# A selective scan run in place over tiles that alternate in direction, with layer norm on ScalarE and GpSimd and the products with C in pairs

## The reference, cut to what matters

```python
xn = (xf - mu) / sqrt(var + EPS) * ln_g + ln_b          # layer norm over 64 channels
xz = x @ in_proj_w.T;  xi, z = split(xz)
u = silu(causal_conv4(xi) + conv_b)
dt, Bm, Cm = split(u @ x_proj_w.T)
delta = softplus(dt * dt_proj_w + dt_proj_b)
for t in range(L):                                      # L = 56 * 56 pixels of an image
    h = h * exp(delta[t] * A) + (delta[t] * u[t]) * B[t]   # h: channels x 16 states
    y[t] = sum over states of h * C[t]
out = x + ((y + u * D) * silu(z)) @ out_proj_w.T
```

## Time and profile before

| | |
|---|---|
| median of 3 runs | 9379.95 us (9377.71 to 9384.65) |
| profiled execution | 9385.57 us, span 9383.8 us |
| busy, share of the span | PE 83%, DVE 74%, ACT 57%, POOL 58% |
| Mamba stage | first scan at 721.2 us, last at 7038.8 us |
| operations of the Mamba loop | 3584 scans, 3584 drives, 3584 decays, 3584 products |
| memset of `hs` ahead of the loop | 6.03 us on VectorE |

### The profile page before, as it was taken

One profiled execution on the slowest core, in us unless ns is written; L12 is line 12 of the kernel. 1 busy time (PEld: TensorE's weight loads), 2 busy tenths in 40 slices (PEclk: granted clock), 3 DMA queues, 4 the chain that ended last, 5 costly groups with the idle time before them and its releaser, 6 DMA issues. The chain is left out here.

```text
span 9383.8 us, 134613 instructions
## 1 busy us (share of the span) xinstructions
PE 7771.6 (83%) x30601; PEld 4082.9 (44%) x30601; DVE 6973.6 (74%) x9361; ACT 5322.5 (57%) x9326; POOL 5475.1 (58%) x4944
## 2 busy tenths in 40 slices
PE   9977777787777778777777777777778999999996
PEld 9962222222222222222222222222225899959996
DVE  7759999999999999999999999999991122212222
ACT  0237777777777777777777777777770133201432
POOL 0008888888888888888898888888880000000000
PEclk9988888888888888788887888888889999999998
DMA  9646565655655656555665565656651000030002
GB/s 175 168 122 167 159 166 162 165 163 162 166 163 165 163 162 166 163 164 164 164 167 162 163 164 165 166 161 166 163 162 56 17 0 0 18 86 0 0 0 55
DMA packets 1108342, 1202.02 MB, mean 128 GB/s; under 512 B 460432, under 2 KB 1094800, under 8 KB 1107344
## 3 DMA queue, kind: packets, MB, share of 16 engines
q1 hardware_dynamic: 871568, 1117.24, 44.2%
q10 hardware_dynamic: 236032, 77.08, 3.6%
HBM read 961.04 MB, written 155.41 MB: 119 GB/s over the span
## 5 line engine op out<-in xcount | busy, mean ns | idle before, releaser
L644 POOL TENSOR_TENSOR prod<-hs,bsp 128x448 f32<-128x448 f32 x3584 | 4067.8, 1158 | 647.1 <-PE ps L655 464.1
L632 DVE TENSOR_TENSOR_SCAN hs<-da,hs,ps 128x448 f32<-128x448 f32 x3072 | 3490.8, 1136 | 0.0
L623 DVE TENSOR_TENSOR ps<-ps,bsp 128x448 f32<-128x448 f32 x3585 | 2186.6, 610 | 249.1 <-PE ps L607 223.0
L607 PE MATMUL ps<-stack,seld 96*128 96x448 bf16 x3587 | 1422.2, 411 | 1054.8 <-DVE hs L632 1001.9
L613 ACT ACTIVATE da<-da,nega 128x448 f32<-128x448 f32 x3588 | 2235.9, 661 | 16.0 <-issue 7.2
L906 PE MATMUL ps<-pv,ws 128*128 128x224 f32 x8800 | 1692.3, 354 | 9.4 <-ACT pv L1064 7.0
L906 PEld LDWEIGHTS ps<-pv,ws 128*128 128x128 f32 x8800 | 1657.3, 189 | 45.0 <-issue 7.7
L655 PE MATMUL ps<-prod,wc 128*32 128x448 f32 x7200 | 1551.4, 719 | 90.3 <-POOL prod L644 86.7
L607 PEld LDWEIGHTS ps<-stack,seld 96*128 96x128 bf16 x3587 | 347.8, 99 | 2660.5 <-DVE hs L632 2338.2
L1237 DVE SCALAR_TENSOR_TENSOR pv<-ps,R 128x224 f32<-128x224 f32 x880 | 422.4, 480 | 1279.0 <-PE ps L906 1279.0
L407 PE MATMUL ps<-xn,wtap 128*128 128x448 f32 x1808 | 982.3, 650 | 3.5 <-ACT bsp L467 3.5
(11 more groups left out here) (118 smaller groups left out, 7223.8 us busy)
## 6 DMA issues: line engine op xcount, KB each, us to landing
da<-delta_copy SPq DMA_DIRECT2D x3595, 224.0 KB, 3.6
stack<-parts SPq DMA_DIRECT2D x2700, 28.0 KB, 2.3
delta_copy<-dlt SPq DMA_DIRECT2D x225, 224.0 KB, 1.9
lnx<-in_x SPq DMA_DIRECT2D x118, 224.0 KB, 3.7
lny<-y_nchw SPq DMA_DIRECT2D x118, 224.0 KB, 4.3
x_column_pairs<-otile SPq DMA_DIRECT2D x225, 116.0 KB, 2.7
xpad<-x_column_pairs SPq DMA_DIRECT2D x32, 812.0 KB, 4.3
xpad<-in_x SPq DMA_DIRECT2D x64, 392.0 KB, 6.8
```

The lines of the kernel that those rows point to most:

```text
L607: pe.matmul(ps[:, DU_BANK + j % 4, 0:T], seld[0:96, b, :], stack[:, st.t % 2, grp, :], start=True, stop=True).then_inc(S["du_spread"], 1)
L623: v.tensor_tensor(du, du, bsp[:, st.t % 2, 0, :], ALU.mult).then_inc(S["dbu_done"], 1)
L632: v.tensor_tensor_scan(hs[:, j, :], da[:, j % SLOTS, :], ps[:, DU_BANK + j % 4, 0:T], 0.0 if first else hs[:, j, T - 1:T], ALU.mult, ALU.add)\
L644: g.tensor_tensor(prod[:, j % 8, :], hs[:, j, :], bsp[:, st.t % 2, 1, :], ALU.mult)\
```

## The change

Four things are changed in the Mamba stage.

1. The scans run in place: `hs` is gone, `da` has 16 slots of 449 columns, and the state takes the place of the decays. Every second tile (odd t) lies backwards in time, so that the last state of a tile is the column next to where the following tile begins. A scan runs over 449 columns from 1.0: its first column takes over the state left by the tile before (a zeroed PSUM column is its drive). What TensorE reads for a backward tile (`xn` for the taps and `z`, `yg` for the projection) is read backwards.
2. A load of decays waits for the product of the same unit in the tile before, not for a scan.
3. Layer norm leaves VectorE: ScalarE applies scale and shift (`ln_affine`), GpSimd adds (`ln_sum`) and multiplies by `rstd` (`ln_scale`), and gain and bias go into ScalarE's last step.
4. GpSimd multiplies two units by C in one instruction, at odd steps; some steps of the tables move.

```diff
-ACT_AT = {2: ["relu", "cast0"], 4: ["cast1"], 5: ["silu", "u", "z", "exp"], 6: ["evacuate"], 7: ["lnc"], 8: ["bc0"],
-          9: ["dt"], 10: ["dt2", "bc1"], 11: ["lnv"], 13: ["clamp"], 14: ["shift"]}
-DVE_AT = {0: ["add_x"], 3: ["gate"], 11: ["scale"]}
-POOL_AT = {1: ["rest0"], 4: ["rest1"], 9: ["over"], 12: ["delta"], 13: ["delta_u"]}
-SP_AT = {1: ["copy"], 7: ["part0"], 10: ["part1"], 12: ["part2"], 13: ["store"]}
+ACT_AT = {0: ["scale_y"], 2: ["cast0"], 3: ["relu"], 4: ["cast1"], 5: ["silu", "u", "z", "exp"], 6: ["evacuate"],
+          7: ["lnc"], 8: ["bc0"], 9: ["dt"], 10: ["dt2", "bc1"], 11: ["lnv"], 13: ["clamp"], 15: ["shift"]}
+DVE_AT = {3: ["gate"]}
+POOL_AT = {1: ["rest0", "add_x"], 5: ["rest1"], 9: ["over"], 11: ["delta"], 13: ["delta_u", "times_rstd"]}
+SP_AT = {1: ["copy"], 5: ["part0"], 7: ["part1"], 9: ["part2"], 12: ["store"]}
...
-            da = sb(m, "da", [P, SLOTS, T])
-            hs = sb(m, "hs", [P, UN, T])
+            da = sb(m, "da", [P, UN, T + 1])
...
+        def span(buf, a, n, back):
+            return buf[:, a + n - 1:a - 1 if a else None:-1] if back else buf[:, a:a + n]
+        def elements(j, t):
+            lo = 0 if t % 2 else 1
+            return da[:, j, lo:lo + T]
+        def drives(bank, lo=1, hi=T + 1):
+            return ps[:, DU_BANK + bank, lo:hi]
...
-                sp.wait_ge(S["x_summed"], st.ln)
+                sp.wait_ge(S["x_relu"], st.ln)
...
-        def ln_sum(v, st):
-            v.wait_ge(S["ln_loaded"], (st.ln + 1) * 32)
-            if not (st.ahead and st.k == 0):
-                v.wait_ge(S["x_relu"], st.ln)
-            v.scalar_tensor_tensor(xsum[:, :], lny[:, :], col(SCALE2), lnx[:, :], ALU.mult, ALU.add)\
-                .then_inc(S["x_summed"], 1)
+        def ln_affine(a, st):
+            a.wait_ge(S["ln_loaded"], (st.ln + 1) * 32)
+            a.activation(lny[:, :], lny[:, :], ACT.Identity, bias=col(SHIFT2), scale=col(SCALE2)).then_inc(S["y_scaled"], 1)
+        def ln_sum(g, st):
+            g.wait_ge(S["y_scaled"], st.ln + 1)
+            g.tensor_tensor(lnx[:, :], lnx[:, :], lny[:, :], ALU.add).then_inc(S["x_summed"], 1)
...
-            a.activation(xres[:, :], xsum[:, :], ACT.Relu, bias=col(SHIFT2)).then_inc(S["x_relu"], 1)
+            a.activation(xres[:, :], lnx[:, :], ACT.Relu).then_inc(S["x_relu"], 1)
...
-            v.scalar_tensor_tensor(xg[:, :], xcen[:, :], vec_c(0), xrstd[:, :], ALU.mult, ALU.mult)\
-                .then_inc(S["scaled"], 1)
+        def ln_scale(g, st):
+            g.wait_ge(S["rstd"], st.ln + 1)
+            g.tensor_tensor(xcen[:, :], xcen[:, :], xrstd[:, :], ALU.mult).then_inc(S["scaled"], 1)
...
-                sp.wait_ge(S["scan_done"], (st.tile - 1) * UN + (j + 9))
+                sp.wait_ge(S["prod_done"], st.tile * UN + (j + 1))
...
-            v.wait_ge(S["prod_done"], n + 1)
-            first = st.t % KT == 0
-            v.tensor_tensor_scan(hs[:, j, :], da[:, j % SLOTS, :], ps[:, DU_BANK + j % 4, 0:T],
-                                 0.0 if first else hs[:, j, T - 1:T], ALU.mult, ALU.add)\
-                .then_inc(S["scan_done"], 1)
+            h, bank = da[:, j, :], j % 4
+            if st.t == 0:
+                a, d, start = h[:, 1:T + 1], drives(bank), 0.0
+            elif st.t == KT:
+                a, d, start = h[:, T - 1::-1], drives(bank, 1, T + 1)[:, ::-1], 0.0
+            elif st.t % 2:
+                a, d, start = h[:, ::-1], drives(bank, 1, T + 2)[:, ::-1], 1.0
+            else:
+                a, d, start = h, drives(bank, 0, T + 1), 1.0
+            v.tensor_tensor_scan(a, a, d, start, ALU.mult, ALU.add).then_inc(S["scan_done"], 1)
...
-            g.wait_ge(S["scan_done"], n + 9)
+            g.wait_ge(S["scan_done"], n + 10)
...
-            g.tensor_tensor(prod[:, j % 8, :], hs[:, j, :], bsp[:, st.t % 2, 1, :], ALU.mult)\
-                .then_inc(S["prod_done"], 1)
+            lo = 0 if st.t % 2 else 1
+            g.tensor_tensor(prod[:, j % 8:j % 8 + 2, :], da[:, j:j + 2, lo:lo + T],
+                            bsp[:, st.t % 2, 1:2, :].to_broadcast([P, 2, T]), ALU.mult).then_inc(S["prod_done"], 2)
...
-                        times_c(g, st, j)
+                        if j % 2:
+                            times_c(g, st, j - 1)
```

More of the change, by code:

```diff
@@ L192, in build @@
             "y_summed", "y_gated", "out_mm", "out_evac", "out_stored0", "out_stored1")}
-        spread_in = [sem(f"c_spread_in{i}") for i in range(SLOTS)]
+        spread_in = [sem(f"c_spread_in{i}") for i in range(16)]
         D = {n: sem("d_" + n) for n in (
@@ L406, in conv_tap @@
             a = st.far_k * T + k
-            mm = pe.matmul(ps[:, TMP_BANK + bank, 0:T], wtap[:, st.far_s, k, :], xn[:, a:a + T],
+            mm = pe.matmul(ps[:, TMP_BANK + bank, 0:T], wtap[:, st.far_s, k, :], span(xn, a, T, st.back),
                            start=(k == 0), stop=(k == 3))
@@ L415, in emit @@
                     a = st.far_k * T + 3
-                    return pe.matmul(o, wcs("gate_in", st.far_s, P), xn[:, a:a + T], start=True, stop=True)
+                    return pe.matmul(o, wcs("gate_in", st.far_s, P), span(xn, a, T, st.back), start=True, stop=True)
             elif name == "dt":
@@ L606, in spread_du @@
             pe.wait_ge(S["scan_done"], st.tile * UN + j + 5)
[L607 removed]
+            pe.matmul(drives(j % 4), seld[0:96, b, :], stack[:, st.t % 2, grp, :],
                       start=True, stop=True).then_inc(S["du_spread"], 1)
         def decay(a, st, j):
[L612 to L613 removed]
+            a.wait_ge(spread_in[j], st.tile * 16 + 16)
+            a.activation(elements(j, st.t), elements(j, st.t), ACT.Exp, scale=nega[:, j:j + 1])\
                 .then_inc(S["exp_done"], 1)
@@ L671, in project_out @@
                 o = ps[lo:lo + C, O_BANK, 0:T // 2]
-                pe.matmul(o, wcs("proj_out", 0, C), yg[:, odd:T:2], start=True, stop=False)
+                y = yg[:, T - 1 - odd:None if odd else 0:-2] if back else yg[:, odd:T:2]
+                pe.matmul(o, wcs("proj_out", 0, C), y, start=True, stop=False)
                 mm = pe.matmul(o, wcs("residual", s, C), xn[:, 3 + k * T + odd:3 + k * T + T:2], start=False, stop=True)
@@ L857, in _ @@
             sum_states(pe, tile, 3)
-            project_out(pe, tile, s, k)
+            project_out(pe, tile, s, k, par == 1)
             barrier(pe, 3)
@@ L1010, in _ @@
                                 evacuate(a, tile, par, before)
+                            elif name == "scale_y":
+                                if st.has_ln:
+                                    ln_affine(a, st)
                             elif name == "relu":
@@ L1117, in _ @@
                 v.sem_inc(S[f"out_stored{par}"], 16)
-            for k in range(6):
-                st = Ahead(k)
-                ln_sum(v, st)
-                ln_scale(v, st)
             for j in range(LEAD["drive"]):
@@ L1131, in _ @@
                         for name in DVE_AT.get(j, ()):
-                            if name == "gate":
-                                gate(v, tile, ub)
-                            elif name == "add_x":
-                                if st.has_ln:
-                                    ln_sum(v, st)
-                            elif st.has_ln:
-                                ln_scale(v, st)
+                            gate(v, tile, ub)
             tile, ub, s, k, par, before, img = ended(PAIRS, 0)
@@ L1254, in _ @@
             g.wait_ge(S["ready"], 4)
+            for k in range(6):
+                st = Ahead(k)
+                ln_sum(g, st)
+                ln_scale(g, st)
             st = Ahead(0)
@@ L1275, in _ @@
                                 delta_times_u(g, st)
-                            else:
+                            elif name.startswith("rest"):
                                 rest_of(g, st, int(name[4]))
+                            elif st.has_ln:
+                                if name == "add_x":
+                                    ln_sum(g, st)
+                                else:
+                                    ln_scale(g, st)
             barrier(g, 3)
```

34 lines of the change are left out of this document (14 added, 20 removed).

## The result

The changed kernel takes 9417.4 us (median of 7; 9409.3 to 9432.1), the kernel before beside it 9384.7 us: a ratio of 1.0037 (95% interval 1.0025 to 1.0049). It is slower, by 33 us where I had forecast 190.

A forecast was written before the change was run, and what follows sets the result against it. It took a ring of waits between ScalarE and GpSimd as the bound: seven plain tiles at 26.1 and seven layer-norm tiles at 32.0 us, +11.6 a pair of images, +192 with the start, about 9570 us (9404 to 9748).

The forecast's parts named there:

- The ring: ScalarE and GpSimd, in program order, wait for each other: 12.24 us cast to `over`, 14.28 back, setting a tile without layer norm.
- plain tile: Tile without layer norm, seven in a pair of images; forecast 26.1 us with four pairs of products, a gain of 0.5.
- layer-norm tile: One of tiles 8 to 13 and 0; forecast 32.0 us against 29.9 before, a loss of 2.1.
- relu to cast: ScalarE's relu, the decay behind it and a handoff, newly on the ring in layer-norm tiles: 1.2 us.
- One sign: Expected in the profile if right: ScalarE's relu waiting some 5 us for GpSimd's `add_x`.
- q = 2.10: Price in us of one GpSimd instruction multiplying two units: two products at 1.10 less a fixed part; bounds 1.96 and 2.32.
- the upper side: Reasons for a pair price near 2.32 us: the pair's second dimension and its starts at odd columns.
- 304.3 + 49q: Time in us of a pair of images as a function of q, the price of a pair of products.
- Item 3: Layer-norm tile, from the end of `dq` to `delta` by TensorE's sum, two pairs and `over`: 4.35 us, lower bound 3.8.
- rival 4: Gain and loss cancel, q near 1.85 to 1.9, no change in time; chance 0.04.
- Backward scans: Rival: backward scans or drives are dear, 1.30 us instead of 1.075, a backward tile 28.3, kernel 9710; chance 0.08.
- the rival had 8615: Rival: VectorE sets the end after all, every tile takes its 24.8 us, kernel 8615; chance 0.05.

The follow-up runs named there:

- b_const: The kernel before with every scan started from 0.0, so no state is carried from tile to tile; 9368.7 us, ratio to before 0.9984.
- a_best: a_early with a separate buffer for the scaled chunk, GpSimd's product by rstd after unit 3 and ScalarE's shift after unit 14; 9039.5 us, ratio to before 0.9626.
- a_dt_relu: a_dt with ScalarE's relu moved from unit 9 to unit 6, ahead of `dt`; 8680.4 us, ratio to before 0.9249.
- a_unroll: The changed kernel with two pairs of images in one pass of the loop, 8 passes in place of 16; 9387.6 us.
- a_late: The changed kernel with GpSimd's product by rstd and ScalarE's shift one tile later; 9383.9 us, ratio to before 1.0002.
- a_early: a_late with `scale_y`, `add_x` and SP's loads for them one tile earlier; 9362.8 us, ratio to before 0.998.
- a_lnv: The changed kernel with layer norm back on VectorE, scans and pairs as in the change; 9387.2 us, ratio to before 1.0001.
- a_lnv_late: a_lnv with VectorE's scaling and ScalarE's shift one tile later; 9266.9 us, ratio to before 0.9875.
- a_dt: a_best with work on `dt` ahead of layer norm's relu, centring and squares, `scale_y` and `add_x` back in the relu's tile; 9026.3 us, ratio to before 0.9611.
- a_single: The changed kernel with one GpSimd product an instruction instead of pairs; 9491.1 us, ratio to before 1.0114.
- a_forms: The changed kernel plus GpSimd products of several shapes timed on zeros ahead of the loop; one row 1126 ns, two rows 2068 ns.

## Why the prediction was wrong in size

**The ring was right.** Cast to `over` 12.25 us (12.24 forecast); plain tile 17.72 + 4 × 1.90 = 25.3 against 25.4 measured. In the layer-norm tile shown: relu to cast 1.05 (1.2), cast to the end of `dq` 13.6 (13.5), from there to `delta` 3.8 (4.35; 4.3 in the tile before it). From the end of the squares to the first pair behind TensorE's sum it took 3795.08 − 3790.35 = 4.73 us, against 4.74 before. b_const, a_best and a_dt_relu show the mechanism by taking it apart: cheaper scans bought 16 us, another order of the same work 737. As a sum the ring is less sure: a_unroll, a_best and a_dt_relu came out near what it gave (a_dt_relu 35 us below), while a_late, a_early, a_lnv, a_lnv_late and a_dt gained 79 to 213 us less, and a_single cost 161 less. One sign came out weak: the relu waits 1.7 to 1.9 us for `add_x`, where I had named some 5; the long wait is GpSimd's 6.92 for the sum.

**The step that failed is the price of the pair, q = 2.10.** Its pitch is 1.90 (3.65 to 3.98 for two), below even my lower bound of 1.96. The parts, from runs: two products at 1.10 are 2.21; one fixed part less, 184 ns where I took 98 from a memset; and 0.15 less because one row of a pair, on average, starts at a cheap column, a saving of the new layout for which I had no term. 2.21 − 0.18 − 0.15 = 1.88. The repeated row of C, my reason for a low bound, brings nothing, and the odd starts, one of my reasons for the upper side, are what makes half the rows cheaper.

**Two more errors, which nearly cancel.** The forecast's formula, 304.3 + 49q, gives 397.4 us a pair of images at 1.90, close to the 396.6 measured, and 49 × 0.20 × 16 = 157 us is close to the 153 by which the time was missed. That closeness is luck. Item 3 of the forecast holds the price of two further pairs, which the formula leaves at 2.10; at 1.90 the item is 3.95, a layer-norm tile 31.05 and a pair of images 7 × 25.32 + 7 × 31.05 = 394.6, against 394.9 in the mean before: no change. Tiles 8 to 13 bear this out with 30.91. What made the kernel slower is tile 0, 33.06 for 31.05: ScalarE's wait at the loop's jump, which the sum put at nothing (a_unroll, 31.13 without the jump). 2.0 × 16 = 32 us, of the 33 measured; the rest cancels within a few microseconds, the start among it (4.8 us for 7). So the time lies within my range of 9404 to 9748 by luck, too. It lies nearest to rival 4, no change with q at 1.85 to 1.9, which I gave 0.04.

**The count of pairs is too large as a rule.** Going back to single products raises the price by 0.14 us a pair; over 49 pairs that should cost 110 us, over 63 (with item 3's) 141. It cost 74, in the main because in the layer-norm tiles `over`, and so the sum that it stands behind, came sooner (a_single). The agreement above holds for the waits of this kernel alone.

**The rivals.** Backward scans are not dear: 1078 ns in both directions. VectorE's floor of 24.8 us a tile is real, but only another order reaches it: a_dt_relu comes to 8680 where the rival had 8615. The rule of the Trainium skill, Perfetto Trace Analysis, section "Identifying the Most-Contended Engine", would have begun with VectorE, the busiest engine of the plain tiles before. b_const disagrees, 26.45 us a plain tile with cheaper scans.

## What to carry to other kernels

When two engines that work in program order hand work back and forth inside a tile, write down the ring and price what lies on it; the busy shares say little until the ring is broken. A step that is moved off the ring brings its own waits to the place where it lands, so look at what its input waits for there. Price a merged instruction by measuring the fixed part on that engine, and look at what the new layout does to the price, too: sort the times of one instruction by row before taking their mean.

## What the runs showed of the hardware

- GpSimd multiplies a row of 448 columns that starts at a multiple of four columns in 1126 to 1134 ns (a_forms, before); a straight line through 224 and 448 columns leaves 186 ns of it fixed. A row that starts two or three columns behind a multiple of four takes 977 ns (a_single). Two rows in one instruction take 1770, 1927 or 2080 ns with two, one or none of the cheap kind (after).
- VectorE's scaling, with two SBUF inputs, takes 653 ns in the median where it is placed after unit 5 (a_lnv_late) and 1965 ns where it meets GpSimd's pairs (a_lnv); in one such tile it ended 0.5 us after the pair. Its longest was 1689 ns among single products (before) and 2337 among pairs. The Trainium skill, SBUF — State Buffer, section "Who interferes with whom", describes an exclusive lock on a pair of ports that VectorE and GpSimd share. These rows agree with it: the excess over 683 ns, 1.01 and 1.65 us, stays under one product and one pair.
- ScalarE's first instruction after the loop's jump came 3.84 us late in the pass shown, 3.2 in the mean of the 15 jumps (after), with no releaser in the profile; each jump saved gave 3.7 us (a_unroll).
